# Two graph attentions: ScalarE's relu and exp on the first two PSUM banks together, in two pieces per unit instead of three, and in another order

## The reference

```
e = leaky_relu(a1[src] + a2[dst], 0.2)          # one number per edge
m = segment_max(e, dst);  w = exp(e - m[dst])
out = segment_sum(w * feat[src], dst) / segment_sum(w, dst)
```

## Time and profile before

| | |
|---|---|
| median of 3 runs | 3988.24 us (3983.79 to 3988.59) |
| the profiled execution | 3962.7 us, span 3961.1 us |
| granted TensorE clock, mean over the span | 0.969 |
| busy over the span | PE 92%, PEld 75%, DVE 50%, ACT 42%, POOL 39% |
| first attention | first relu 617.1 us, last exp and weighing before 1103 us |
| second attention | first to last weighing 1660.3 to 2052.6 us |

### The profile page before, as it was taken

How to read it: one execution, slowest core, us unless ns; L and a number is a source line. 1 busy time by engine, 2 the same in 40 slices (tenths; PEclk the granted TensorE clock), 3 DMA queues, 4 the chain that set the end, 5 groups by cost and what they waited for, 6 DMA issues and landing times.

```text
span 3961.1 us, 58218 instructions
## 1 busy us (share of the span) xinstructions
PE 3625.3 (92%) x18463; PEld 2970.5 (75%) x18473; DVE 1961.6 (50%) x2783; ACT 1682.3 (42%) x2911; POOL 1556.8 (39%) x1168
## 2 busy tenths in 40 slices
PE   8998868999978897589989999999999999989998
PEld 4555437999978897333336999999999999955598
DVE  7245788888533635899955323333322231023334
ACT  1113677888832321499971333333333333300020
POOL 3887886666600001000001444444444444367500
PEclk9999998999989998799999999999999999999999
DMA  4343112232233302311024555555555553379801
GB/s 147 98 112 74 45 23 62 78 90 78 71 114 100 119 20 82 115 40 40 33 73 138 186 183 187 186 183 175 175 183 185 188 183 112 102 274 305 247 9 63
DMA packets 176460, 483.10 MB, mean 122 GB/s; under 512 B 40798, under 2 KB 57205, under 8 KB 176342
## 3 DMA queue, kind: packets, MB, share of 16 engines
q1 hardware_dynamic: 87414, 201.95, 15.7%
q0 software_dynamic: 54368, 185.24, 15.3%
q10 hardware_dynamic: 34560, 94.45, 6.7%
HBM read 357.64 MB, written 123.55 MB: 121 GB/s over the span
## 4 chain that ended last, share of the span: by engine, by line
PE 40%; ACT 7%; POOL 5%; issue 3%; DVE 2%; DMA 1%; SPq 0%; DVEq 0%; ACTq 0%; POOLq 0%
PE ps L1893 30%; POOL work L1975 5%; ACT work L1279 3%; PE ps L1881 3%; ACT ps L1270 3%; PE ps L1558 3%; PE ps L306 2%; PE ps L298 1%; DVE work L1101 1%; PE ps L1216 1%; DVE work L1129 0%; DMA work<-msg_d,work 0%; ACT work L1289 0%; DMA ct<-x_d 0%; PE ps L324 0%
## 5 line engine op out<-in xcount | busy, mean ns | idle before, releaser
L1893 PE MATMUL ps<-wsplit,xsplit 128*128 x6840 | 1236.9, 337 | 2.7 <-DVEq L1833 2.7
L1893 PEld LDWEIGHTS ps<-wsplit,xsplit 128*128 128x128 f32 x6840 | 1181.5, 188 | 2.9 <-issue 2.9
L1830 DVE CAST wsplit<-wplain 128x768 fp32r<-128x768 f32 x204 | 117.1, 574 | 759.6 <-PE ps L1893 744.3
L1860 POOL TENSOR_TENSOR xsplit<-ct,xsplit 128x768 fp32r<-128x768 f32 x190 | 369.9, 1947 | 296.6 <-ACTq L1925 296.6
L1279 ACT ACTIVATE work<-ps,work 128x418 f32<-128x418 f32 x720 | 437.7, 631 | 107.7 <-PE ps L1189 102.3
L1930 ACT ACTIVATE ct<-ps,invs 128x768 f32<-128x768 f32 x190 | 171.4, 902 | 713.1 <-PE ps L1893 713.1
L1226 PE MATMUL ps<-hbuf,work 128*128 128x193 f32 x2400 | 455.2, 328 | 15.4 <-DVE work L1143 13.1
L1226 PEld LDWEIGHTS ps<-hbuf,work 128*128 128x128 f32 x2400 | 407.4, 190 | 43.4 <-issue 16.9
L1270 ACT ACTIVATE ps<-work,lr 128x418 f32<-128x418 f32 x720 | 431.4, 633 | 6.0 <-DMA work<-lrow_d 6.0
L1129 DVE SCALAR_TENSOR_TENSOR work<-work,cnt 128x1250 f32<-128x1250 f32 x240 | 349.9, 1458 | 133.3 <-ACT work L1279 132.7
L1855 POOL DMA_INDIRECT ct<-x_d,relrec x190 | 200.5, 1055 | 455.9 <-PE ps L1881 448.3
(11 more groups left out here) (212 smaller groups left out, 4399.8 us busy)
## 6 DMA issues: line engine op xcount, KB each, us to landing
wplain<-in_L_gnn_W_rel SPq DMA_DIRECT2D x34, 2304.0 KB, 9.7
msg_d<-ct ACTq DMA_DIRECT2D x190, 384.0 KB, 2.6
work<-lrow_d SPq DMA_DIRECT2D x47, 625.0 KB, 3.7
feat_d<-work ACTq DMA_DIRECT2D x30, 386.0 KB, 4.3
hbuf<-feat_d SPq DMA_DIRECT2D x60, 193.0 KB, 2.5
gat_d<-work POOLq DMA_DIRECT2D x12, 960.0 KB, 5.2
xplain<-gat_d SPq DMA_DIRECT2D x30, 384.0 KB, 3.2
work<-xa_d SPq DMA_DIRECT2D x27, 384.0 KB, 3.5
```

Of the source, the lines that this page charges most:

```text
L1860: g.tensor_tensor(xlo7[:, k % XW, :], xt7[:, k % 2].rearrange("p c n -> p (c n)"), xhi7[:, k % XW, :].bitcast(F32), ALU.subtract).then_inc ...
L1893: last = pe.matmul(ps[:, 4 + 2 * (u % 2) + h, 0:HALF], x[:, u, c * P:(c + 1) * P], w[:, bass.ds(base + (c * D + h * HALF), HALF)], start=( ...
```

## The change

ScalarE's work of a unit is cut into two pieces: banks 0 and 1 together (836 targets, as 2 x 418 elements in one instruction), and bank 2 (414 targets). The order per unit becomes exponent(q, 0), relu(q, 1), relu(q + 1, 0), exponent(q, 1), where piece 0 is the wide one; in att2 the copies of the sums stand behind the first three. The relu and exp of piece 0 raise their semaphores by two. TensorE still adds bank by bank. In att0 the adds of banks 0 and 1 both stand behind the products of tile 1 and that of bank 2 behind tile 6 (before 1, 4 and 7); in att2 both stand behind the first product of 512 targets and that of bank 2 behind the third product. VectorE, the DMAs and the buffers are the same.

```diff
--- before.py
+++ after.py
@@ -960,7 +960,8 @@
-            H, CUTS = 12, [(0, 418), (418, 834), (834, N)]
+            H, CUTS = 12, [(0, 418), (418, 836), (836, N)]
+            PIECES = [(0, 2), (2, 3)]
             AHEAD = 4
             def __init__(self, C, mask, columns, outs, isolated):
@@ -1215,7 +1216,10 @@
                                 pe.wait_ge(self.s_flat, 3 * (h - 1) + k + 1)
                             last = pe.matmul(ps[0:C + 1, 3 + k, 0:n1 - n0], self.feat(h, s), p[:, n0:n1], start=(s == 0), stop=(s == NT - 1))
                             last.then_inc(self.s_agg, 1)
-                            adds[k]()
+                            if k == 0:
+                                adds[0]()
+                                adds[1]()
+                        adds[2]()
                         if s == 1 and h:
                             turn_back(h - 1)
                         return
@@ -1227,8 +1231,11 @@
                                          start=(s == 0 and t == 0), stop=(s == NT - 1), skip_group_check=True)
                         if dt == NT - 1:
                             last.then_inc(self.s_agg, 1)
-                        if dt in (1, 4, 7):
-                            adds[dt // 3]()
+                        if dt == 1:
+                            adds[0]()
+                            adds[1]()
+                        if dt == 6:
+                            adds[2]()
                 for q in range(2):
                     for piece in add(q):
@@ -1257,27 +1264,37 @@
             def act(self, act):
                 H = self.H
+                def piece(b):
+                    b0, b1 = self.PIECES[b]
+                    c0, c1 = self.CUTS[b0][0], self.CUTS[b1 - 1][1]
+                    return ps[:, b0:b1, 0:(c1 - c0) // (b1 - b0)], c0, c1, b1
+                def banks(row, b):
+                    return row.rearrange("p (b n) -> p b n", b=2 if b == 0 else 1)
                 def relu(q, b):
                     if q >= NT * H:
                         return
                     h, s = divmod(q, NT)
-                    c0, c1 = self.CUTS[b]
+                    at, c0, c1, done = piece(b)
                     if s == 0 and b == 0:
                         act.wait_ge(self.s_R[h % 2], self.at["r_row"] + 16 * (h // 2 + 1))
                     col = self.columns[h][0] + s
                     if q:
-                        act.wait_ge(self.s_exp, self.at["exp"] + 3 * (q - 1) + b + 1)
-                    act.activation(ps[:, b, 0:c1 - c0], self.Rb[h % 2][:, c0:c1], ACT.Relu, bias=lr[:, col:col + 1]).then_inc(self.s_relu, 1)
+                        act.wait_ge(self.s_exp, self.at["exp"] + 3 * (q - 1) + done)
+                    act.activation(at, banks(self.Rb[h % 2][:, c0:c1], b), ACT.Relu, bias=lr[:, col:col + 1]).then_inc(self.s_relu, 2 - b)
                 def exponent(q, b):
                     h, s = divmod(q, NT)
-                    c0, c1 = self.CUTS[b]
+                    at, c0, c1, done = piece(b)
                     col = self.columns[h][0] + s
                     if b == 0 and q >= 3:
                         act.wait_ge(self.s_agg, self.at["agg"] + (3 if self.narrow else 1) * (q - 2))
-                    act.wait_ge(self.s_add, self.at["add"] + 3 * q + b + 1)
-                    act.activation(self.p[q % 3][:, c0:c1], ps[:, b, 0:c1 - c0], ACT.Exp, bias=self.l2[:, col:col + 1], scale=1.0 - SLOPE)\
-                       .then_inc(self.s_exp, 1)
+                    act.wait_ge(self.s_add, self.at["add"] + 3 * q + done)
+                    act.activation(banks(self.p[q % 3][:, c0:c1], b), at, ACT.Exp, bias=self.l2[:, col:col + 1], scale=1.0 - SLOPE)\
+                       .then_inc(self.s_exp, 2 - b)
                 def sums_out(h, k):
@@ -1290,22 +1307,19 @@
                 act.wait_ge(self.s_primed, 6 if self.narrow else 3)
                 act.wait_ge(self.s_cols, self.at["cols"] + 1)
-                for b in range(3):
-                    relu(0, b)
+                relu(0, 0)
                 for q in range(NT * H):
                     turn = self.narrow and q >= NT and q % NT == 1
                     exponent(q, 0)
                     if turn:
                         sums_out(q // NT - 1, 0)
-                    exponent(q, 1)
+                    relu(q, 1)
+                    if turn:
+                        sums_out(q // NT - 1, 1)
                     relu(q + 1, 0)
                     if turn:
-                        sums_out(q // NT - 1, 1)
-                    exponent(q, 2)
-                    if turn:
                         sums_out(q // NT - 1, 2)
-                    relu(q + 1, 1)
-                    relu(q + 1, 2)
+                    exponent(q, 1)
                 if self.narrow:
                     for k in range(3):
                         sums_out(H - 1, k)
```

## The result

The changed kernel took 4088.8 us (median of 4 runs, 4082.2 to 4096.6) beside 3988.2 us of the kernel before: ratio 1.0256, 95% interval 1.0243 to 1.0268. That is 101 us slower where 34 were forecast, and above the range. The profiled execution took 4094.98 us (span 4093.4). First the stretches of the two attentions, as the earlier trace rows: start and end, busy us (count) of PE, PEld, DVE, ACT and POOL, the granted clock of TensorE, DMA share, GB/s.

The account below looks back on a forecast made before the run. The prediction took TensorE to bound the first attention and ScalarE the second. A new loop through both engines would add 19 and 15 us, together 34, to 3988.24 us: 4022 us, range 3992 to 4045.

Parts of the forecast that it names:

- ScalarE alone: Both attentions: four ScalarE instructions a unit instead of six, 2.76 us in sum, 0.31 less than 3.07.
- The loop: Adds, wide exp, narrow relu, third add, products, next adds: 3.97 us a unit against 3.80 (first attention), 3.19 against 3.07 (second).
- The sum: Whole kernel: first attention 19 us longer, second 15 us (heads 33.7 us instead of 32.4), together 34 us.
- the sum's first term: First attention: 113 units each 0.17 us longer through the loop, 19 us.
- a lower granted clock: TensorE, both attentions: listed as a sign of a wrong forecast; 1.00 before, and no term held it.
- The base: Whole kernel: median 3988.24 us is 0.6% above the profiled 3962.7, and the same was added to the forecast.
- Rivals 1 and 2: Both attentions: 1, loop doesn't close, ScalarE's saving comes through, 3969 us, chance 0.10; 2, about nothing, 3988 us, chance 0.10.
- Rival 3: Heads' turns: copies, transposes, shifts and division each come whole on the loop, 20 us on top, 4042 us, chance 0.16.

Follow-up runs that it names:

- e3: Changed kernel with the first attention's third add behind tile 8 instead of tile 6: 3982.6 us, 1.0057 of the kernel before.
- e8: Changed kernel, gathers moved out of the first attention, second attention's third add one product earlier: 4054.7 us beside 3962.9 (one run).
- e10: Kernel before with two pieces and the pair of adds ahead of a unit's products in the second attention alone: 3958.5 us, 0.9985.
- e11: The changed kernel itself, run again on quiet chip 0: 4006.0 us, 1.0107 of the kernel before at 3963.7.
- e5: Changed kernel with the first attention's gathers paced to two for each weighing, on a quiet chip: 4003.7 us, 1.0107 of the kernel before.
- e9: Changed kernel with three gathers released for each weighing, on a quiet chip: 4003.5 us beside 3963.7 (one run).
- e15: The kernel of e5 (changed kernel, two gathers a unit) again, on quiet chip 8: 4003.5 us, 1.0099 of the kernel before.
- e12: The changed kernel itself, run again on disturbed chip 7: 4095.2 us beside 3985.8 for the kernel before (one run).
- e13: Changed kernel with the gathers moved out of the first attention, on disturbed chip 7: 4244.4 us beside 3985.8 (one run).
- e18: Changed kernel with the first attention's gathers paced to two a unit, on disturbed chip 10: 4028.2 us, 1.0098 of the kernel before.
- e19: The kernel of e10 (kernel before, second attention alone with two pieces and adds first) on disturbed chip 10: 3980.8 us, 0.9979.
- e1: Changed kernel with the gathers moved out of the first attention into later stages, on a quiet chip: 4007.6 us, 1.0121 of the kernel before.
- e4: Changed kernel with the first attention's third add behind tile 8 and the gathers moved out, on a quiet chip: 3986.0 us, 1.0062.
- e6: Changed kernel with 8 of 16 gathers a head beside the first attention, the rest behind it, on a quiet chip: 3999.9 us, 1.0098.

## Why the prediction was wrong, point by point

- **ScalarE alone.** Right: wide instructions 0.96 us, 0.85 before the follower.
- **The loop.** Right in each term: exp 0.64 behind the adds (0.62), 3.97 and 3.19 to 3.20 us a unit. e3, e8 and e10 show the cause, each undoing or lengthening one link.
- **The sum.** First attention 471.1 to 490.8 us on a quiet chip: 19.7 (19 forecast). Second 392.2 to 408.4: 16.2 (15), heads 33.77 (33.7). The 15 is near in part by luck: all heads were taken as 32.4 us before, and the last two are shorter (30.2 and 28.4). Heads 1 to 9 gained 1.36 us each (1.3 forecast), head 0 0.6, head 10 1.9 and head 11 1.4 (0.9 forecast for the last two). The whole, e11 beside its own kernel before: 42 us for 34. The other 6 or so lie ahead of the first attention and between the two: these stretches are 5 to 8 us longer in e5, e9, e11 and e15 than in the kernel before, and no run shows why.
- **What failed** is the sum's first term: the first attention was 113 x 0.17 = 19 us and nothing else, at full clock. The sum went through the instructions of TensorE, ScalarE and VectorE, and never asked what GpSimd's gathers do when the unit grows: two a unit became three. On the disturbed chips the first attention then costs 557.1 - 490.8 = 66 us more, and 20 + 66 + 16 = 102 us for the two attentions stand beside the 101 measured. e12 and e13 show that the gathers do it; that it is their rate is only made likely by e18. The one sentence that pointed there, on a lower granted clock "which no term here holds", was not followed up.
- **The base.** The 0.6% from the profile (3962.7) to the median (3988.24) was carried over as a factor. It has a place: the profile is that of a quiet chip, the medians those of a disturbed one, and the 25 us lie in the last stage (1908.6 us behind the second attention, against 1933.3 to 1935.1 in all five traces from disturbed chips). There they fall into the stretch of the last 196 gathers (work<-msg_d): from the first to the last 251.5 us in the kernel before on a quiet chip, 279.7 in e19. The kernel before itself has no trace on a disturbed chip, so for it this is by its shared code, not seen.
- **The rivals.** None had the result. Rivals 1 and 2 needed a loop of no more than about 3.8 and 3.1 us; it is 3.97 and 3.2. Rival 3 (turns that stack) did not happen: heads of 33.77 us. On a quiet chip the mechanism and nearly the size would have been right. The range was made from terms of one mechanism alone, with nothing for what shared the stretch.

Open: what makes a chip disturbed, and by what path a gather holds up another engine's signal and TensorE's issue. One lead is in the traces: each gather makes 16 increments of its semaphore, 3040 in all, and the kernel waits for every one of them before it goes on. Quiet chips' traces hold nearly all (3040 in the kernel before, 3030 in e11). Those of disturbed chips lack many: 898 are left in the trace of the result and 899 in e12, but also, with hardly a pause, 2156 in e18 and 1862 in e19. So the recording loses events there, and the pauses may be of the recording's making: the executions timed here give span and clock from such records, so no run tells what an unrecorded one does. The Trainium skill (NOTIFIC — the notification-queue block, section Overflow: three behaviours, one of which stalls the engine) says that the block that writes such records, when a ring of it is full, by its setting drops the new record, overwrites the oldest or holds up whoever produces them. Missing records would fit the first two and held-up engines the third; no run here shows which of them, or whether any, is at work. Nor was the changed kernel run at three a unit on e18's chip; on chip 7 and in the session of the result it paused.

## What to carry to other kernels

When instructions of two engines are merged or reordered, walk the ring of waits through both engines once, with what is queued behind each waiting instruction; a merge on one engine pays only if no other engine's long work lies between the merged result and its next use (here: adds ahead of the products, or the third add late). When a loop's unit changes length, count again what the other queues start in it, above all small DMAs that nothing paces; pacing them to the work cost nothing here (e5, e15) and no pause was seen with it (e18). And before an experiment on a rare disturbance is believed, run the disturbed kernel itself beside it: e1, e4, e5 and e6 here "cured" pauses that, by the times of the kernel before, their chips did not have.

## What the runs showed of the hardware

- Small gathers from GpSimd, three in a unit of 3.97 us, hold up other engines' semaphore increments on some chips, in most heads by up to 4.4 us and by 7.2 at most (the result; e12 alike), and leave no trace on others (e11, e9). The 320 indirect DMAs of L767 ahead of the first attention show no such loss on either kind: it begins at 623.0 to 629.6 us on quiet and at 624.2 to 628.9 on disturbed chips. At 1.25 us apart and 120 in a row, TensorE went on by one instruction in 1.40 us, with waits of up to 103 us behind it; at two in 3.97 us nothing was held up (e18), nor at 16 in 22.3 us in one head of e19 on the same chip.
- The pause comes late in a burst: the gathers of the head shown begin at 914.41, the first held-up exp is at 931.91.
- A pause costs twice: 4 us of idle TensorE, then in ten heads of eleven half the clock, ten records in 3.42 us for 1.79.
- On the disturbed chips the traces lack semaphore events of the gathers: 70% where the core paused (the result, e12), 29% and 39% where it hardly did (e18, e19), under 1% on quiet chips. So a count of events tells such a chip, but not whether the core paused.
- The kernel before differs by 25 us (0.6%) between chips, put down above to the last stage by the traces of its relatives.
- Two banks in one ScalarE instruction cost elements alone: 836 elements 0.96 us, 0.35 more than 418.
